# Tables for the next turn of items fetched between the items of this one, in a second register set; eight-word table rows; two copies and a clearing moved

## The reference

```python
def _sage_layer(x, src, dst, Wl_i, bl_i, Wr_i):
    msg = x[src]
    agg = segment_sum(msg, dst, num_segments=6250)
    cnt = segment_sum(ones, dst, num_segments=6250)
    return agg / clip(cnt, 1.0)[:, None] @ Wl_i + bl_i + x @ Wr_i
...
z = concatenate([x[dst], x[src], edge_attr], axis=-1)
msg = sigmoid(z @ Wf.T + bf) * softplus(z @ Ws.T + bs)
agg = segment_sum(msg, dst, num_segments=6250)
...
x = layernorm(x + sage(x)); x = layernorm(x + conv(x))
```

## Time and profile before

| | us |
|---|---|
| median of three runs | 3432.28 (3430.3 to 3433.51) |
| the profiled execution's own time | 3432.11 |
| its span, first to last instruction | 3430.4 |
| PE busy | 2659.0 |
| POOL busy | 2346.7 |
| DVE busy | 2137.3 |
| ACT busy | 1224.4 |

### The profile page before, as it was taken

The page is one execution under the profiler, slowest core; times in us unless marked ns, Lnnn a source line. Parts: engine busy times, 40 slices in busy tenths (PEclk is TensorE's granted clock), DMA queues, the critical chain, the costliest instruction groups (busy, mean ns, idle before and its releaser), DMA issues.

```text
span 3430.4 us, 69755 instructions
## 1 busy us (share of the span) xinstructions
PE 2659.0 (78%) x16221; PEld 1989.6 (58%) x16222; DVE 2137.3 (62%) x4942; ACT 1224.4 (36%) x1682; POOL 2346.7 (68%) x2399
## 2 busy tenths in 40 slices
PE   6578888675887875757888856688888888888874
PEld 6345555574655555645655556556666666666654
DVE  6635445466432224566544556778888888888886
ACT  2423333011000000110000002267888888888866
POOL 3667777576777777767777777467777777776610
PEclk8789999897999997878998978999999999999997
DMA  5354444323655562237777643344444444444411
GB/s 156 100 189 148 130 148 130 96 74 105 174 158 143 148 160 51 73 102 230 235 239 220 195 115 109 90 138 126 127 125 127 126 127 126 126 117 117 115 52 38
DMA packets 346021, 454.93 MB, mean 133 GB/s; under 512 B 135643, under 2 KB 260599, under 8 KB 342311
## 3 DMA queue, kind: packets, MB, share of 16 engines
q0 software_dynamic: 88624, 207.58, 22.5%
q10 hardware_dynamic: 127520, 197.33, 18.0%
q1 hardware_dynamic: 129768, 48.71, 5.8%
HBM read 357.03 MB, written 101.90 MB: 134 GB/s over the span
## 4 chain that ended last, share of the span: by engine, by line
POOL 35%; PE 20%; issue 20%; DVE 10%; DMA 9%; DVEq 2%; SPq 2%; ACT 2%; POOLq 0%; ACTq 0%
POOL shared L762 26%; POOL shared L802 9%; DMA shared<-q_dram,idx 6%; PE ps L957 6%; PE ps L948 4%; PE ps L1188 3%; PE ps L940 2%; SPq L637 1%; DVE work L2377 1%; DVE work L2060 1%; PE ps L967 1%; DMA dense_dram<-work 1%; ACT work L1521 1%; PE ps L1207 1%; PE ps L1191 1%
## 5 line engine op out<-in xcount | busy, mean ns | idle before, releaser
L762 POOL DMA_INDIRECT shared<-y_even,idx x1056 | 1039.4, 984 | 399.0 <-issue 311.5
L802 POOL DMA_INDIRECT shared<-q_dram,idx x784 | 779.1, 994 | 282.3 <-issue 224.5
L948 PE MATMUL ps<-shared,work 128*128 x4368 | 665.2, 301 | 324.4 <-SPq L598 194.2
L948 PEld LDWEIGHTS ps<-shared,work 128*128 128x128 f32 x4368 | 605.6, 211 | 400.0 <-issue 388.6
L2087 DVE TENSOR_TENSOR acc<-acc,ps 128x129 f32 x546 | 155.3, 284 | 848.3 <-PE ps L948 654.4
L762 POOL DMA_INDIRECT shared<-y_odd,idx x528 | 511.1, 968 | 178.1 <-issue 159.7
L1188 PE MATMUL ps<-pq,work 128*128 x1664 | 502.1, 404 | 142.6 <-issue 96.9
L2377 DVE TENSOR_TENSOR work<-ps,shared 128x256 f32<-128x256 f32 x832 | 294.5, 416 | 174.5 <-PE ps L1191 148.7
L1188 PEld LDWEIGHTS ps<-pq,work 128*128 128x128 f32 x1664 | 259.3, 196 | 237.8 <-issue 167.8
L967 PE MATMUL ps<-pq,work 128*128 128x385 bf16 x1456 | 296.1, 354 | 61.2 <-DVE work L2074 24.2
L1375 ACT CAST work<-ps 128x600 bf16<-128x600 f32 x260 | 159.6, 662 | 340.7 <-PE ps L940 314.8
(11 more groups left out here) (368 smaller groups left out, 3883.0 us busy)
## 6 DMA issues: line engine op xcount, KB each, us to landing
work<-counts_dram ACTq DMA_DIRECT2D x156, 384.0 KB
counts_dram<-work ACTq DMA_DIRECT2D x26, 1568.0 KB
ea_parts<-work ACTq DMA_DIRECT2D x128, 196.0 KB
ea_sb<-ea_parts SPq DMA_DIRECT2D x196, 128.0 KB
work<-counts_dram ACTq DMA_DIRECT2D x52, 416.0 KB
shared<-y_even,idx POOLq DMA_INDIRECT x1056
shared<-q_dram,idx POOLq DMA_INDIRECT x784
shared<-y_odd,idx POOLq DMA_INDIRECT x528
```

Of the source, the lines that this page charges most:

```text
L762: pool.indirect_dma_start(msg[:, u, 0:F], None, y_two[layer % 2], bass.IndirectOffsetOnAxis(ap=idx[:, u:u + 1], axis=0)).then_inc(s_quad[q ...
L802: pool.indirect_dma_start(q_ring[:, u * 2 * F:(u + 1) * 2 * F], None, q_dram, bass.IndirectOffsetOnAxis(ap=idx[:, u:u + 1], axis=0)).then_ ...
L948: last = te.matmul(ps[:, SUM_BANKS[i], 0:FA], lhsT=oh4[:, OH_SLOTS[i], u, :], rhs=shared[:, bass.ds(place + u * FA, FA)], start=u == 0, st ...
```

## The change

1. **Fetching.** PE and DVE have two sets of each table register. `load_turn` and `load_pairs` are gone. The rows for the next turn are read between the items of this one: after items 1, 2, 3 and 4 a load of four words each (`fetch_beside`), in the turns with pairs two more on PE (after pair items 0 and 5) and four on DVE. A turn begins with registers that are full. Rows for a layer's first turn and first turn with pairs are read ahead of them.
2. **Eight-word rows.** Every load is of four words, also the second half of a row, which before had three. The DMAs that write the rows bring eight words for each turn. SP's `needed` in the convolution also reads four and four.
3. **Copies.** The two halves of the attribute copy leave the place after turn 0 of layer 0 and stand ahead of SP's last two turns of twelve quads there (before quads 108 and 120).
4. **Clearing.** `acc` is cleared by ACT, a chunk after its norm (the last after Q is written), not by POOL after the last gather.
5. **load_x** waits for the load before it, not for its own.

```diff
-            def copy_sorted():
+            def copy_attributes(h):
                 with sp.If(unsorted < 1):
-                    for h in range(2):
-                        sp.dma_start(eaT_sorted[:, h * EP // 2:(h + 1) * EP // 2],
-                                     eaT[:, h * EP // 2:(h + 1) * EP // 2]).then_inc(s["ea_sorted"], 16)
+                    sp.dma_start(eaT_sorted[:, h * EP // 2:(h + 1) * EP // 2],
+                                 eaT[:, h * EP // 2:(h + 1) * EP // 2]).then_inc(s["ea_sorted"], 16)
...
                 turn(0)
-                if not layer:
-                    copy_sorted()
-                with sp.Fori(1, QG // RQ - 1) as it:
+                with sp.Fori(1, QG // RQ - 2) as it:
                     turn(it)
-                turn(QG // RQ - 1)
+                for h in range(2):
+                    if not layer:
+                        copy_attributes(h)
+                    turn(QG // RQ - 2 + h)
...
-            with pool.Fori(0, NCH) as it:
-                pool.wait_ge(s["var_z"], it + 1)
-                gp.tensor_copy(acc[:, bass.ds(it * (CW * FA), CW * FA)], zero[:, :].to_broadcast([P, CW * FA]))\
-                    .then_inc(s["acc_clear"], 1)
...
+                def fetch(it, of, part):
+                    k = part % 2 * 4
+                    if part < 2:
+                        pe.reg_load(t_regs[k:k + 4], q_regs[0:1, bass.ds(it * WIDE + (NEEDED_AT + k), 4)])
+                        for i in range(k, min(k + 4, IT)):
+                            pe.reg_alu(q_sets[of][i], t_regs[i], 1, ALU.max)
+                            if layer:
+                                pe.reg_alu(q_sets[of][i], q_sets[of][i], layer * QG, ALU.add)
+                    else:
+                        pe.reg_load(g_sets[of][k:k + 4], q_regs[0:1, bass.ds(it * WIDE + (PLACES_AT + k), 4)])
+
+                def fetch_beside(it, of, i):
+                    if i in (1, 2, 3, 4):
+                        fetch(it, of, i - 1)
...
                         for half_ in range(2):
-                            places = load_turn(m * 2 + half_)
+                            places = places_in(half_)
                             for i in range(IT):
                                 counts_before(m, half_ * IT + i, COUNTS_AT)
-                                item(m * 2 + half_, i, places[i])
+                                item(m * 2 + half_, i, places[i], half_)
+                                fetch_beside(m * 2 + half_ + 1, 1 - half_, i)
...
             def load_x(c):
+                if c:
+                    act.wait_ge(s["x_in"], c * 16)
+                alone(act)
                 act.dma_start(y_again[c % 2], xv[:, c * CW:(c + 1) * CW, :]).then_inc(s["x_in"], 16)
-                act.wait_ge(s["x_in"], (c + 1) * 16)
...
+            def clear_sums(it):
+                sc.copy(acc[:, it * (CW * FA):(it + 1) * (CW * FA)], zero[:, :].to_broadcast([P, CW * FA])).then_inc(s["acc_clear"], 1)
...
                 if it < 2:
                     next_x(NCH - 2 + it)
+                if it < NCH - 1:
+                    clear_sums(it)
                 copy_x1(it)
                 copy_q(it)
+            clear_sums(NCH - 1)
```

More of the change, by code:

```diff
@@ L629, in _ @@
             sp.wait_ge(s["p_done"], (NCH - 1) * 4 + 4)
-            n_regs = [sp.alloc_register(f"sp_n{q}") for q in range(RC)]
+            n_regs = [sp.alloc_register(f"sp_n{q}") for q in range(WIDE)]
             done_regs = [sp.alloc_register(f"sp_d{q}") for q in range(RC)]
@@ L921, in sage_sums, with fetch_pairs, places_in @@
                 alone(pe)
[L923 to L931, removed]
+                def fetch(it, of, part):
[8 more added lines that the diff above has]
+                        pe.reg_load(g_sets[of][k:k + 4], q_regs[0:1, bass.ds(it * WIDE + (PLACES_AT + k), 4)])
+                def fetch_pairs(turn, of, part):
+                    k = part * 4
+                    pe.reg_load(d_sets[of][k:k + 4], q_regs[0:1, bass.ds(turn * WIDE + (PLACES_AT + TURNS * WIDE + k), 4)])
+                def fetch_beside(it, of, i):
+                    if i in (1, 2, 3, 4):
+                        fetch(it, of, i - 1)
+                def places_in(of):
+                    return [pe.snap(r, min_val=0, max_val=(RQ - 1) * QT * FA) for r in g_sets[of][0:IT]]
                 def count(n, k, slot):
@@ L969, in multiply_piece, with pairs_in @@
                     last.then_inc(s["counted"], 1)
[L971 to L974 removed]
+                def pairs_in(of):
+                    return [pe.snap(r, min_val=0, max_val=(NGR - PT) * FA) for r in d_sets[of][0:IT]]
                 def pair_item(turn, i, place):
@@ L991, in counts_before @@
                         count(m * (3 * GT), k, k % CSLOT)
+                for part in range(4):
+                    fetch(0, 0, part)
                 if layer:
@@ L2217, in sage_adds @@
                 ready_to_split(layer)
-                columns = load_columns(FIRST_COLS_AT, OHS - 1)
+                for part in range(4):
+                    fetch(0, 0, part)
+                columns = first_columns(FIRST_COLS_AT, OHS - 1)
                 for i in range(OHS - 1):
@@ L2239, in sage_adds @@
                         add_item(layer, WOVEN - 1, i, sums, columns)
+                        fetch_beside(WOVEN, 1, i)
                 first_pairs(layer)
+                for part in range(4):
+                    fetch_pairs(0, 1, part)
                 def both(b, residual=None, ending=None, conv=False):
-                    sums, columns = load_turn(b + WOVEN)
-                    p_sums, p_columns = load_pairs(b)
+                    mine, other = (b + 1) % 2, b % 2
+                    sums, columns = turn_in(mine)
+                    p_sums, p_columns = pairs_in(mine)
                     for i in range(IT):
@@ L2248, in both @@
                         dve.wait_ge(s["added_items"], b * IT + (WOVEN * IT + layer * NI1 + i + 1 + OHS))
+                        if b + 1 < DTURNS:
+                            fetch_beside(b + 1 + WOVEN, other, i)
                         add_pair(layer, b, i, p_sums, p_columns)
+                        if b + 1 < DTURNS and i in (0, 2, 4, 5):
+                            fetch_pairs(b + 1, other, (0, 2, 4, 5).index(i))
                         if residual is not None and i in (1, 4):
```

123 lines of the change are left out of this document (71 added, 52 removed).

## The result

The changed kernel takes 3374.67 us (median of four runs, 3371.54 to 3383.16) against 3432.88 (3430.30 to 3433.51): a ratio of 0.9836, 95% interval 0.9817 to 0.9854. That is 58.2 us less; forecast were 58, to 3374. The profiled execution took 3374.32, with a span of 3372.5 against 3430.4 before.

A forecast was written before the change was run, and what follows sets the result against it. POOL's gathers bound the kernel, except where POOL waits for PE in layer 0 and where PE, DVE and ACT finish layer 2. Gains of 41 + 2 + 15 = 58 us from 3432.1 gave 3374, range 3354 to 3399.

The forecast's parts named there:

- Layer 0 gains 41: Layer 0: PE saves 57.9 us (gaps, clock, copies, read-back loads), less 17 for 68 half-hidden fetches; layer ends 41 earlier.
- POOL's 42: Layer 0: the most POOL can win, 39.4 us of index waits plus at most 2.8 before the first quad.
- Three words against four: PE's table loads: 0.33 us for four words, about 0.77 for three; eight-word rows save 0.4 on every second load.
- DVE's fetches: DVE, all turns: more in number, but slack in the woven turns; cost set to 0.
- The copies: Layer 0, after the first turn: moving the attribute copies takes away PE's 16.1 us wait.
- Their new place: Late layer 0: index transfers behind each moved copy are hidden; cost taken as 0, up to 12 us each otherwise.
- The second rival: Late layer 0: the moved copies are not covered and gathered rows land late; 3386 to 3398 us, chance 0.12.
- The end of layer 2: Last gather to last item of layer 2: sum 24 less 9 for PE's fetches, 15 us of a possible 17.5.
- 11.5 + 3 + 4.9 + 4.6: End of layer 2: turn heads 11.5, half-clock items 3, ACT's x waits 4.9, DVE's one-hot blocked by clearing 4.6; 24 us.
- unhidden fetches: First rival, PE in layers 0 and 2: nothing of a 0.48 us fetch is hidden; 3398 us, chance 0.15.
- long loads in the stream: Third rival, PE's fetches between items: loads of 1.01 us, nothing hidden; slower by 23, 3455 us, chance 0.03.
- POOL used what it was given: Opposite of the fourth rival, where other waits replace POOL's index waits and nothing is won: 3432 us, chance 0.02.

The follow-up runs named there:

- pe_doubled: The changed kernel with each PE fetch preceded by a second load of the same four words into other registers, one of them used: 3381.29 us.
- rows_only: The kernel before with eight-word rows, so every table load is of four words, all loads still at the turn heads: 3404.41 us.
- dve_doubled: The changed kernel with each DVE fetch preceded by a second load of the same four words into other registers, one of them used: 3379.74 us.
- copies_only: The kernel before with only the two attribute copies moved to the last two turns of twelve quads of layer 0: 3415.32 us.
- copies_back: The changed kernel with both attribute copies back in their old place behind the first twelve quads of layer 0: 3383.41 us.
- fetch_of_three: The changed kernel with the second half of each table row fetched by a three-word load on PE and DVE: 3384.39 us.
- no_fetch: The changed kernel without the fetching: one register set and all loads at the turn heads, all other parts kept: 3378.96 us.
- pe_heads: The changed kernel with PE's loads gathered behind the last item of each turn, still into the second set, DVE still fetching between items: 3404.14 us.

## Why the prediction was right, point by point

*What bounds the kernel* held. What was won, was won in the two places where POOL or the end waited for PE; layers 1 and 2 up to their last turns and the convolution moved by less than 2 us each.

*Layer 0 gains 41* was right in size (39.8) by a step that was mis-sized, and so in part by luck. I took PE's gain as the bound, with half of each fetch exposed, 0.25 us. PE starts turn 17 639.8 - 590.8 = 49.0 earlier, where gaps, clock, copies and the loads behind the read-back were priced at 57.9. So 68 fetches cost at most 8.9, 0.13 each, not 17. Part of the 8.9 belongs to the clock, whose 10 us were too many: over five passes PE was busy 252.98 us before and 248.70 after, which makes some 7 in the 8.5 passes, and leaves about 0.09 for a fetch. The bound was then the other one I had named, POOL's 42, of which it took 38.3 in the window to 645 us and 1.4 of the 2.8 ahead of it. That the two stood only 1 us apart hid the error. pe_doubled shows that the cover is thin: the next 0.37 us of a fetch costs 0.2. The Trainium skill, "DMA: Bandwidth & Descriptors", section "Latency and other measured facts", gives a register load a floor of about 600 ns. The runs contradict it with 327 ns for four words; by the page's figure, an estimate, a fetch would be 0.27 us longer, three quarters of the step to pe_doubled.

*Three words against four* was right in its price on PE (0.77 to 0.33) and too small in its reach. I counted it for PE and set DVE to 0. DVE had the same loads, and rows_only won 17.9 at the end of layer 2 with heads that still stood there; PE's waits for DVE fell by 7.2 in it. *DVE's fetches*, set to 0, cost next to nothing in the woven turns, but doubled they cost 8.7 us at the end of layer 2 (dve_doubled): there DVE has no slack to spare.

*The copies*: 16.1 forecast, 16.3 measured in copies_only. *Their new place* costs 0, as taken: the last 24 quads take 124.1 us from first gather to last, as before (647.3 to 771.4, 687.1 to 811.2), and 122.9 in copies_back, without copies there. The second rival is out. POOL could issue 16 gathers in 20 us beside the copy, whose data came at 0.34 MB in 11 us instead of 0.59. The Trainium skill, "DMA: Bandwidth & Descriptors", section "Queues, rings and completion order", has a DMA engine alternate between queues packet by packet; the trace agrees in that the gathers were slowed and not stopped.

*The end of layer 2*: 15 forecast, 17.1 measured. The 17.5 that I took for the most is no sharp limit: rows_only won 17.9 and fetch_of_three 18.8. But the terms of the sum (11.5 + 3 + 4.9 + 4.6) are not pieces that add up. Each part alone reaches into the same allowance: the rows alone win 17.9, clearing and `load_x` alone 11.9, and undoing them costs nothing. The claim that the blocked one-hot lies on the way of the items is refuted for this state: in rows_only it takes 5.70 us and the last item is 5.2 us behind the gather.

*The rivals*: unhidden fetches are out by the pass of 52.8; long loads in the stream occur (1147 ns at the longest) and are few; POOL used what it was given. What I did not ask is what each edit is worth beside the others. The fetching, the change's largest edit, wins 4 us in layer 0; the eight-word rows had brought PE's pass from 56.7 to 54.3, already under POOL's 55.5.

*Left open*: whether the fetching is worth more than the 4 us of layer 0. Of the rest of the 8.6 us between no_fetch and the change 2.9 lie behind the last item, where the two kernels don't differ, and 8.6 is twice what two medians of one program differ by. Why copies_only shortened the end of layer 2, and how rows_only's gain there divides between PE and DVE, wasn't tried either.

## What to carry to other kernels

Write the rate of the engine that bounds a stretch beside the rate of the one it waits for: from the point where the second is faster, further savings there buy nothing, and edits that share the allowance can't be priced by adding their single gains. Before moving register loads out of the way, look at their lengths: padding a row so that each load is four words won 29.2 us here without any load being moved. Beside all the other edits the padding was worth 9.7 to 14.0 us (fetch_of_three) and the hiding 4.3 to 8.6 (no_fetch); hiding alone wasn't run. Four loads in a row were free here where long work was queued ahead of them on their engine and cost their whole length where little was, so the place in the stream can matter more than the number.

## What the runs showed of the hardware

A load of three words into registers took a median of 0.77 us on PE and 0.75 on DVE, one of four 0.33 to 0.34 and 0.35, in each run that had both. On the DVE line that loads the windows the longest was 3.09 us before and 1.17 in rows_only. Four loads of four words in a row cost PE 2.31 us behind an item of eight matmuls (pe_heads) and no idle time behind a multiply of 49 (no_fetch). Beside a copy that kept the DMA engines 0.72 busy gathers went on at 0.34 MB in 11 us, against 0.59 without it. The granted clock, 0.97 on average through the woven turns with gaps of 2.7 us between turns, was 1.00 without them.
